# Cross-scan layers: the softplus difference formed by TensorE, its positive part taken by ScalarE from PSUM, skip products in the first order, u exchanged by ScalarE

## The reference

```python
xin, z = split(x @ in_proj.T)                      # 192 channels each
x_hw, x_wh = rows of xin, the same with h and w exchanged
xs = [x_hw, x_wh, flip(x_hw), flip(x_wh)]          # 4 sequences of length 1024
dts, Bs, Cs = x_proj[k] @ xs[k]                    # 12 + 16 + 16 rows
delta = softplus(dt_proj[k] @ dts + bias[k])
h[t] = exp(delta[t] * A) * h[t-1] + delta[t] * B[t] * u[t]      # 16 states a channel
y[t] = sum over states of h[t] * C[t]  +  u[t] * D
y = sum of the 4 sequences, put back in place
out = (layernorm(y) * w + b) * silu(z) @ out_proj.T
```

## Time and profile before

| what | value |
|---|---|
| median of 3 runs | 3590.24 us (3587.51 to 3597.89) |
| profiled execution, its own time | 3596.97 us |
| its span in the profile | 3595.1 us |
| busy: TensorE, VectorE | 2717.0 us (76%), 2981.3 us (83%) |
| busy: ScalarE, GpSimd | 2027.2 us (56%), 2825.5 us (79%) |
| TensorE's granted clock, mean | 0.802 of full |

### The profile page before, as it was taken

How to read it: one execution, slowest core, us unless ns; L and a number is a source line. 1 busy time by engine, 2 the same in 40 slices (tenths; PEclk the granted TensorE clock), 3 DMA queues, 4 the chain that set the end, 5 groups by cost and what they waited for, 6 DMA issues and landing times. The chain is left out here.

```text
span 3595.1 us, 27498 instructions
## 1 busy us (share of the span) xinstructions
PE 2717.0 (76%) x5948; PEld 626.7 (17%) x5948; DVE 2981.3 (83%) x1934; ACT 2027.2 (56%) x2262; POOL 2825.5 (79%) x1212
## 2 busy tenths in 40 slices
PE   5669877887888698245667676778878886988787
PEld 2111111111111111111111112111111111111111
DVE  1899899899989897675988932998999898989994
ACT  3566565657565664313655524656665656656563
POOL 0899999999999997003666613999999999989994
PEclk9778887888788777667789778879887887878787
DMA  2655656473755554103443403574637555555643
GB/s 48 163 136 139 143 137 156 124 169 100 175 137 141 136 144 111 30 0 89 124 107 83 118 1 85 138 172 123 162 107 169 135 138 137 138 138 135 160 121 96
DMA packets 140881, 437.19 MB, mean 122 GB/s; under 512 B 33909, under 2 KB 34619, under 8 KB 140395
## 3 DMA queue, kind: packets, MB, share of 16 engines
q1 hardware_dynamic: 140714, 435.58, 50.1%
HBM read 307.56 MB, written 6.82 MB: 87 GB/s over the span
## 5 line engine op out<-in xcount | busy, mean ns | idle before, releaser
L881 POOL TENSOR_TENSOR L_read<-L_state,L_c_rows 128x1024 f32<-128x1024 f32 x768 | 1799.6, 2363 | 103.2 <-DVE L_state L989 90.0
L671 PE MATMUL L_y_ps<-L_read,L_fold 128*64 128x512 f32 x3072 | 1230.1, 905 | 312.1 <-POOL L_read L881 311.2
L868 POOL TENSOR_TENSOR L_state<-L_du,L_b_rows 128x1024 f32<-128x1024 f32 x256 | 605.3, 2364 | 26.6 <-POOL L_read L881 3.9
L989 DVE TENSOR_TENSOR_SCAN L_state<-L_decay,L_work_ps 128x1024 f32<-128x1024 f32 x256 | 585.3, 2286 | 26.7 <-DVE L_work_ps L970 2.5
L989 DVE TENSOR_TENSOR_SCAN L_state<-L_work_ps,L_state 128x1024 f32<-128x1024 f32 x256 | 581.2, 2270 | 29.8 <-POOL L_state L868 21.3
L814 ACT ACTIVATE L_work_ps<-L_delta,L_a_neg 128x1024 f32<-128x1024 f32 x256 | 286.3, 1118 | 562.4 <-DVE L_state L989 562.3
L989 DVE TENSOR_TENSOR_SCAN L_state<-L_decay,L_row_ps 128x1024 f32<-128x1024 f32 x256 | 585.4, 2287 | 8.8
L814 ACT ACTIVATE L_decay<-L_delta,L_a_neg 128x1024 f32<-128x1024 f32 x512 | 584.3, 1141 | 12.9 <-DVE L_state L989 6.1
L970 DVE TENSOR_TENSOR L_work_ps<-L_du,L_row_ps 128x1024 f32<-128x1024 f32 x256 | 314.3, 1228 | 214.4 <-issue 147.0
L671 PEld LDWEIGHTS L_y_ps<-L_read,L_fold 128*64 128x64 f32 x3072 | 191.2, 157 | 1190.1 <-POOL L_read L881 747.1
L1519 POOL TENSOR_TENSOR L_read<-L_state,L_c_rows 128x1024 f32<-128x1024 f32 x96 | 237.1, 2470 | 165.7 <-DVE L_state L1625 139.5
(11 more groups left out here) (323 smaller groups left out, 2897.7 us busy)
## 6 DMA issues: line engine op xcount, KB each, us to landing
L_b_rows<-L_bc_dram SPq DMA_DIRECT2D x580, 256.0 KB, 4.2
L_c_rows<-L_bc_dram SPq DMA_DIRECT2D x580, 256.0 KB, 4.0
L_delta<-L_delta SPq DMA_DIRECT2D x204, 256.0 KB, 5.9
L_du<-L_du SPq DMA_DIRECT2D x140, 256.0 KB, 6.2
L_du<-L_u SPq DMA_DIRECT2D x64, 256.0 KB, 6.0
L_bc_dram<-L_dbl SPq DMA_DIRECT2D x40, 128.0 KB, 3.4
L_delta<-L_delta_a SPq DMA_DIRECT2D x16, 256.0 KB, 4.4
L_du<-L_du_a SPq DMA_DIRECT2D x16, 256.0 KB, 5.1
```

The costliest lines, as they stand in the source:

```text
L671: m = nc.tensor.matmul(y_ps[i * BLK:(i + 1) * BLK, c, :], fold[:, :], y_half(t, o, i), start=first, stop=last, skip_group_check=True)
L868: nc.gpsimd.tensor_tensor(state[:, last, :], du2[:, d * NBLK + last, :], b_rows[:, g % 2, :], ALU.mult).then_inc(injected_c, 1)
L881: nc.gpsimd.tensor_tensor(read[:, t % READS, :], state[:, t % STATES, :], c_rows[:, g % 2, :], ALU.mult).then_inc(multiplied, 1)
L989: nc.vector.tensor_tensor_scan(state[:, c, way], by[:, way], fed[:, way], 0.0, ALU.mult, ALU.add).then_inc(scanned, 1)
```

## The change

GpSimd's `gap` goes away with its semaphore and its table. TensorE forms the difference as a new side of two products ("gap": more by the identity, l by minus the identity), ScalarE takes its positive part from PSUM into l, in two halves, in place of the ReLU over the whole row in SBUF. The u side reads g as it lies in both orders, and ScalarE writes u with h and w exchanged for the second order. The skip products move to tiles 2, 3 and 4 of the first order and read u as it lies. The tables of sides and of ScalarE's softplus steps are written anew, SiLU moves from tile 43 to 42, and the head runs the new sides in the order of PREPARE[1].

```diff
-FINISH = [{("cent", 0): (1, 3), ("cent", 1): (4,), ("var", 0): (10, 11), ("out", 0): (15, 16)},
-          {("z", 0): (36, 37), ("z", 1): (38, 39), ("shift", 0): (43, 44)}]
...
-POOL_GAP = [{24: 0, 30: 1, 36: 2}, {18: 0, 25: 1, 31: 2}]
...
-SILU_AT, RSTD_AT, Y_AT, ADD_AT = 43, 16, 1, 21
+FINISH = [{("cent", 0): (1, 3), ("cent", 1): (4,), ("var", 0): (10, 11), ("out", 0): (14, 15)},
+          {("z", 0): (35, 36), ("z", 1): (37, 38), ("shift", 0): (43, 44)}]
+PREPARE = [{("u", 0): (6, 7), ("u", 1): (8, 9), ("bc", 0): (12, 13), ("dt", 0): (17, 18), ("dt", 1): (19, 20),
+            ("dt", 2): (21, 22), ("u", 2): (23, 24), ("gap", 0): (25, 26), ("sum", 0): (28, 29), ("gap", 1): (30, 31),
+            ("sum", 1): (33, 34), ("gap", 2): (35, 36), ("sum", 2): (38, 40)},
+           {("u", 0): (1, 2), ("u", 1): (3, 4), ("bc", 0): (5, 6), ("dt", 0): (8, 9), ("dt", 1): (10, 11),
+            ("dt", 2): (12, 13), ("gap", 0): (15, 16), ("u", 2): (17, 18), ("gap", 1): (20, 21), ("sum", 0): (22, 23),
+            ("gap", 2): (25, 26), ("sum", 1): (27, 29), ("sum", 2): (31, 33)}]
+ACT_SOFTPLUS = [{("exp", 0): 23, ("log", 0): 24, ("one", 0): 25, ("less", 0): 26, ("exp", 1): 27, ("log", 1): 28,
+                 ("one", 1): 30, ("less", 1): 31, ("exp", 2): 32, ("log", 2): 33, ("one", 2): 35, ("less", 2): 36},
+                {("exp", 0): 13, ("log", 0): 14, ("one", 0): 15, ("less", 0): 16, ("exp", 1): 17, ("log", 1): 18,
+                 ("one", 1): 20, ("less", 1): 21, ("exp", 2): 22, ("log", 2): 23, ("one", 2): 25, ("less", 2): 26}]
+SILU_AT, RSTD_AT, Y_AT, ADD_AT = 42, 16, 1, 21
-CROSS_SKIP_AT = (0, 1, 2)
+CROSS_SKIP_AT = (2, 3, 4)
...
-            def g_half(image, order, i):
-                img = g_cm[:, bass.ts(image, L)]
-                if order == 0:
-                    return img[:, i * HALF:(i + 1) * HALF]
-                return img.rearrange("p (h w) -> p w h", w=W)[:, i * (W // 2):(i + 1) * (W // 2), :]
+            def g_half(image, i):
+                return g_cm[:, bass.ts(image, L)][:, i * HALF:(i + 1) * HALF]
...
+                elif kind == "gap":
+                    pe.wait_ge(sp_log, turn.next * NJ + j + 1)
+                    pe.wait_ge(sp_less, turn.next * NJ + j + 1)
+                    parts = [(ident, more[:, s]), (minus_w[:, :], l_of[j][:, s])]
                 elif kind == "sum":
-                    pe.wait_ge(sp_relu, turn.next * NJ + j + 1)
+                    wait_side(pe, turn.use(("gap", j), 1))
...
-                    if o == 1 and t in CROSS_SKIP_AT:
+                    if o == 0 and t in CROSS_SKIP_AT:
...
-                                             y_half(u[rows:rows + BLK, j, :], o, i), start=False, stop=False,
+                                             u[rows:rows + BLK, j, i * HALF:(i + 1) * HALF], start=False, stop=False,
...
-                    ins = nc.scalar.copy(u[:, j, s], side_ps[:, :])
+                    if turn.next_order == 0:
+                        ins = nc.scalar.copy(u[:, j, s], side_ps[:, :])
+                    else:
+                        turned = u[:, j, :].rearrange("p (w h) -> p h w", h=H)[:, i * (H // 2):(i + 1) * (H // 2), :]
+                        ins = nc.scalar.copy(turned, side_ps[:, :].rearrange("p (h w) -> p h w", w=W))
...
+                elif kind == "gap":
+                    ins = nc.scalar.activation(l_of[j][:, s], side_ps[:, :], ACT.Relu)
...
-                    if j > 0 or not isinstance(turn, Head):
-                        act.wait_ge(sp_gap, n)
+                    if j > 0:
+                        act.wait_ge(side_ready, turn.use(("gap", j - 1), 1) + 1)
...
-                else:
-                    act.wait_ge(sp_gap, n + 1)
-                    nc.scalar.activation(l[:, :], l[:, :], ACT.Relu).then_inc(sp_relu, 1)
...
-            ahead = {0: (("exp", 0), ("log", 0), ("one", 0), ("less", 0), ("exp", 1), ("log", 1), ("relu", 0), ("one", 1),
-                         ("less", 1)),
-                     1: (("exp", 2), ("log", 2), ("relu", 1), ("one", 2), ("less", 2)), 2: (("relu", 2),)}
+            ahead = {0: (("exp", 0), ("log", 0), ("one", 0), ("less", 0), ("exp", 1), ("log", 1)),
+                     1: (("one", 1), ("less", 1), ("exp", 2), ("log", 2)), 2: (("one", 2), ("less", 2))}
             for _, key, i in HEAD_SIDES:
-                if key[0] == "sum" and i == 0:
-                    for kind, j in ahead[key[1]]:
+                take(Head(), key, i)
+                if (key, i) == (("dt", 2), 1):
+                    for kind, j in ahead[0]:
                         softplus(Head(), kind, j)
-                take(Head(), key, i)
+                if key[0] == "gap" and key[1] < 2 and i == 1:
+                    for kind, j in ahead[key[1] + 1]:
+                        softplus(Head(), kind, j)
...
-            def gap(turn, j):
...
-            gap(Head(), 0)
-            gap(Head(), 1)
-            form_du(0)
-            gap(Head(), 2)
-            form_du(1)
-            form_du(2)
+            for j in range(NJ):
+                form_du(j)
```

More of the change, by code:

```diff
@@ L609, in side @@
                 if kind == "u":
-                    parts = [(w_u[:, j * 128:(j + 1) * 128], g_half(turn.next_image, turn.next_order, i))]
+                    parts = [(w_u[:, j * 128:(j + 1) * 128], g_half(turn.next_image, i))]
                 elif kind == "bc":
@@ L617, in side @@
                     parts = [(w_dt[:, turn.next_order, j * 128:(j + 1) * 128], dbl[:, s])]
+                elif kind == "gap":
+                    pe.wait_ge(sp_log, turn.next * NJ + j + 1)
+                    pe.wait_ge(sp_less, turn.next * NJ + j + 1)
+                    parts = [(ident, more[:, s]), (minus_w[:, :], l_of[j][:, s])]
                 elif kind == "sum":
-                    pe.wait_ge(sp_relu, turn.next * NJ + j + 1)
+                    wait_side(pe, turn.use(("gap", j), 1))
                     parts = [(ident, e_of[j][:, s]), (minus_w[:, :], l_of[j][:, s]), (ident, delta[:, j, s])]
                 elif kind == "z":
-                    parts = [(w_z[:, j * 128:(j + 1) * 128], g_half(turn.done_image, 0, i))]
+                    parts = [(w_z[:, j * 128:(j + 1) * 128], g_half(turn.done_image, i))]
                 elif kind == "shift":
@@ L654, in y_half @@
             def y_half(t, o, i):
-                src = read[:, t % READS, :] if isinstance(t, int) else t
+                src = read[:, t % READS, :]
                 if o == 0:
@@ L847, in _ @@
         def _(pool):
-            def gap(turn, j):
-                n = turn.next * NJ + j
-                pool.wait_ge(sp_log, n + 1)
-                pool.wait_ge(sp_less, n + 1)
-                l = l_of[j]
-                nc.gpsimd.tensor_tensor(l[:, :], more[:, :], l[:, :], ALU.subtract).then_inc(sp_gap, 1)
             def add_x(turn):
@@ L884, in turn_of @@
                         add_x(turn)
-                    if t in POOL_GAP[turn.r]:
-                        gap(turn, POOL_GAP[turn.r][t])
             def form_du(j):
```

8 lines of the change are left out of this document (4 added, 4 removed).

## The result

The changed kernel takes 3629.5 us (median of 4 runs, 3625.4 to 3633.7), the kernel before 3588.9 beside it: ratio 1.0124, 95% interval 1.0107 to 1.0141. It is slower, by 40 us; the forecast was 16 less. The profiled execution spans 3631.9 us, 36.8 more than that of before.

The account below looks back on a forecast made before the run. VectorE's work plus its waits was taken to set each turn, GpSimd not the plain bound. Terms summed to -4.7 us an image, -38 for eight, +22 for heads: -16, from 3590.24 to 3574 us, range 3532 to 3612.

Parts of the forecast that it names:

- part 3: ScalarE's denser order ahead of B row copies: row waits +2.6 us an image (bounds 0 and +9), SiLU earlier +1.6.
- part 4: Skip products between first-order centring sides, +0.6 us an image; ScalarE's exchanged copies of u, +0.3.
- part 2: VectorE's waits for TensorE's sum sides fall from 10.1 to 4.5 us an image, -5.6; SP's delta copies charged nothing.
- rival 2: Second order's one side bank makes sum waits 12 instead of 3.6: 3641 us, at half 3608; chance 0.18.
- Parts 1 and 2: GpSimd without the difference: direct wait -2.4, late B row -1.8 us an image; sums no longer late: -5.6.
- rival 3: Exchanged copy of u costs its upper end and holds rows back: +22 us, 3596; chance 0.07.
- Part 5: The heads, where no scan runs: new sides and ScalarE's ops add 11 us a head, +22 for two.
- (1): GpSimd is the bound after all: some 5 to 7 us a turn go, 3500 to 3532 us; chance 0.15.
- (4): More work keeps TensorE's clock at the higher level, sum waits go to 0: -36 us, 3538; chance 0.05.

Follow-up runs that it names:

- the relief alone: Kernel before, GpSimd's read product cut to 64 of 1024 columns at the six tiles where it forms the difference: 3516.0 us, ratio 0.9802.
- part 4 alone: Kernel before with skip products at first-order tiles 2 to 4, u read straight and turned by ScalarE's copy: 3569.6 us, ratio 0.9957.
- dense tables alone: Kernel before with the first order's dt and u sides close together, GpSimd's difference kept: ratio 1.0009.
- first-order tables spread: Changed kernel with the first order's dt, difference and sum sides and softplus steps spread, three tiles a pair: ratio 1.0040 to the kernel before.

## Why the prediction was wrong

**What failed is part 3, "the row waits that were 7.8 - 2.1 = 5.7 come to 8.3", with its +1.6 for SiLU.** The rule behind it held: extras in the two steps ahead of a row copy, 0.67 us for three and a microsecond for each more, gave 1.7 for tiles 23 and 24 (1.84 measured) and 1.7, 0.7 and 0.5 in the second order (1.82, 0.66, 0.57). Its terms were too few and too small: 1.2 where 1.63 came (a turned copy of u stands there and takes 0.46 more than a straight one, for which part 4 had 0.3), 0.4 twice where 0.80 and 0.67 came, 2.7 where SiLU took 3.41, and nothing for the late B rows at tile 39 (0.98) and at tile 0 of the second order (0.50). In the turn shown SP sent tile 39's row at 3212.05, behind eight copies of delta and du, which part 2 had at nothing; whether they made it late no run isolates. And at tile 9 I counted ScalarE's own work, 0.7, where it stood idle behind TensorE: 1.94. With 0.3 left at tile 45 and part 4's 0.3 the prediction had 8.3 + 2.7 + 0.3 + 0.3 = 11.6 an image; it is 16.5. That is 4.9 x 8 = 39 us. The runs show these waits to be the loss: taking them out in three steps gave 16, 30 and 50 us, and all three 2.9 per cent, 7 us of it in the heads, while the work of each engine stayed. Part 3's own upper bound, +9, would have given 3574 + 6.4 x 8 = 3625; the range stopped at 3612 (and the half of rival 2, which it names there, is 3608).

**Parts 1 and 2.** GpSimd's direct wait of 2.4 went; the late B row at tile 45 fell by 1.0 instead of 1.8, and ScalarE's wait for that row's DMA stays. The sums fell by 4.3 (10.4 to 6.0, mean of the turns inside the layers), not 5.6. The sum of the last pair in the second order came free as said (4.33 to 0); sum 1 waits 2.7 where I put 2.0, and sum 0 of the first order, where I had 0.5, 0.6 in the first layer and 1.8 to 2.3 in the second. That TensorE is late here was right, by 1.3 x 8 = 10 us too little. The 0.9 a product behind it was misread: a round of the head holds ScalarE's emptying of the bank too. TensorE's busy time grew by 6 us an image (272.1 to 278.3, with u's reads now cheaper), not by 2 x 11. Taken together the two parts were 9.8 x 8 = 78 us, and the relief alone is worth 71. The size was right, in part by luck: the 4.3 of the last pair's sum stayed there, and other sums came early instead. The waits of part 3 stood on top of it.

**Part 4** had the wrong sign: alone it gives 15 us. I wrote that the skip products lengthened TensorE's queue at the second order's start and drew nothing from it; the row wait of 1.9 at tile 9 went with part 4. In "Advanced Engine Details and Errata", section Memory Cachelines, the Trainium skill says that accesses to ever new lines of SBUF are penalised. The trace agrees: the turned copy takes 1044 against 580 ns. But rival 3's time did not follow in the run with part 4 alone; of the six copies of an image those ahead of tiles 12 and 27 alone show in the changed kernel's row waits (0.21 us, and 0.46 of the 1.63).

**Part 5**: 52.9 - 38.8 = 14 a head, forecast 11 (its six halves of a difference at 2.7 are 16.2, not 16.5). In the second head most of the 3 is TensorE's clock, as the last section shows.

**The rivals.** (1), GpSimd as the bound, was nearer than its 0.15: with the row copies on time its load is worth 80 us, the low end of the 80 to 113 given. The mistake was to weigh VectorE's 2.4 us of waits for it against this rival; the two pace each other, and in the first-order turns of the kernel before the wait for GpSimd was cover for the row waits (the run with dense tables alone). (2) gave the sign but not its reason: the sum waits of the second order did not grow, they fell from 6.9 to 4.4. (4): the granted clock did rise, from 0.81 to 0.86 and 0.88, and the sums were late all the same.

The sum by what was measured, means of all 8 images: -2.6 for GpSimd, -3.9 for sums, +9.3 for rows, and -1.7 left over, most of it waits for decays (-1.0) and at loop branches (-0.5): +1.1, 8.5 in all; with 27 for the heads that is 36, and the spans differ by 36.8.

## What to carry to other kernels

Where an in-order engine hands over something that another waits for each round, list what stands ahead of that hand-over in its queue, the waits for third engines as well as its own work; a change that takes work from one engine can lose all of it to the order in which the rest is taken. A stall that costs nothing today may be covered by an engine that the change relieves, so price a relief by taking the load away alone. And move a chain of pieces through one buffer as a whole: moved singly, its wait goes to the next row.

## What was unexpected of the hardware

In the second layer's head TensorE stood 4.7 us without a product (2199.7 to 2204.5), and the next stretch was granted 0.56 of full clock; it stood 2.6 us again (2213.5 to 2216.1), and the next had 0.50, the level of 1.2 GHz. Afterwards it was back at 2.4 GHz (columns as in the windows above, of the changed kernel):

```profile
2204.50:2208.00 3.50, 3.43 (x5) 1.53 (x6) 0.00 (x0) 1.98 (x2) 0.00 (x0) 0.56 0.00 0
...
2216.10:2221.40 5.30, 5.28 (x7) 2.13 (x7) 0.00 (x0) 0.59 (x1) 0.00 (x0) 0.50 0.00 0
2222.50:2226.20 3.70, 3.70 (x9) 1.25 (x7) 0.00 (x0) 1.30 (x3) 0.00 (x0) 1.00 0.00 0
```

Both times TensorE waited for ScalarE, first ahead of the first difference, then ahead of a half of u, and two products behind the second wait took 1.9 us where they take 1.0. But such a pause does not lower the clock each time: in the run with first-order tables spread, whose heads are the same, TensorE stood 2.65 us at this place too, and the stretch behind it (2203.4 to 2208.6) was granted 1.00. The changed kernel, then that run:

```profile
2216.12 2.07 PE L646 MATMUL L_side_ps<-g_cm,L_w_u 96*128 96x512 f32 x2 [2.65 <-ACT L_u L716]
...
2203.39 1.12 PE L646 MATMUL L_side_ps<-g_cm,L_w_u 96*128 96x512 f32 x2 [2.65 <-ACT L_u L716]
```

That head took 50.2 us instead of 52.9. So of the 3 us by which the second head was dearer than forecast, 2.7 went with this fall of the clock, for which I had put 0.5. The turned copy, which writes SBUF with a stride, takes 1.80 times the straight one, much as TensorE's turned read takes 1.88 times.
